# Two attention layers on one core: layer normalisation's last step and the first layer's low activation part moved from VectorE to GpSimd

## What is computed

```
def _layernorm(x, axis=-1, eps=1e-05):
    m = jnp.mean(x, axis=axis, keepdims=True)
    v = jnp.var(x, axis=axis, keepdims=True)
    return (x - m) / jnp.sqrt(v + eps)
...
    x = _layernorm(x + _L0_gnn_ref(x, adj, L0_gnn_Wq, L0_gnn_bq, L0_gnn_Wk, L0_gnn_bk, L0_gnn_Wv, L0_gnn_bv, L0_gnn_beta), axis=-1)
    x = _layernorm(x + _L1_gnn_ref(x, adj, L1_gnn_Wq, L1_gnn_Wk, L1_gnn_Wv, L1_gnn_bv, L1_gnn_Wo, L1_gnn_bo), axis=-1)
    return x
```

## Time and profile before

| | |
|---|---|
| median of 3 runs | 1102.79 us (1102.42 to 1103.21) |
| the profiled execution | 1102.04 us |
| its span on the core | 1100.2 us |
| busy: PE, DVE, POOL, ACT | 96%, 85%, 48%, 40% of the span |
| granted TensorE clock, mean | 0.992 of full speed |

### The profile page before, as it was taken

The page is one execution under the profiler, slowest core; times in us unless marked ns, Lnnn a source line. Parts: engine busy times, 40 slices in busy tenths (PEclk is TensorE's granted clock), DMA queues, the critical chain, the costliest instruction groups (busy, mean ns, idle before and its releaser), DMA issues.

```text
span 1100.2 us, 38267 instructions
## 1 busy us (share of the span) xinstructions
PE 1061.6 (96%) x16896; PEld 916.5 (83%) x16896; DVE 936.5 (85%) x1642; ACT 445.3 (40%) x713; POOL 529.2 (48%) x454
## 2 busy tenths in 40 slices
PE   6789999999999999999999999999999999999975
PEld 5678888888888888888888888888888888888864
DVE  4468998989989898898989989898998989878786
ACT  4334434433444344444434344343343434444321
POOL 0235554554545445364554645455364544655443
PEclk9899999999999999999999999999999999999998
DMA  8211211202111111211201111111211210010101
GB/s 271 64 40 36 74 31 49 60 20 61 38 43 59 43 38 46 65 38 43 59 30 51 46 40 56 42 42 42 65 38 43 59 41 11 17 36 2 36 29 37
DMA packets 61749, 53.32 MB, mean 48 GB/s; under 512 B 35984, under 2 KB 55440, under 8 KB 61584
## 3 DMA queue, kind: packets, MB, share of 16 engines
q1 hardware_dynamic: 60752, 49.69, 15.3%
q10 hardware_dynamic: 832, 1.18, 0.3%
HBM read 38.28 MB, written 12.58 MB: 46 GB/s over the span
## 4 chain that ended last, share of the span: by engine, by line
PE 90%; DVE 4%; issue 2%; ACT 1%; DMA 1%; POOL 1%; ACTq 0%; POOLq 0%; DVEq 0%
PE ps_u L346 53%; PE ps_s L363 9%; PE ps_o L346 8%; PE ps_p L431 7%; PE ps_p L446 7%; PE ps_x L376 3%; PE ps_o L460 2%; DVE probs L628 1%; POOL probs L766 1%; DMA k_sb<-in_wk 1%; DVE row_sum L678 1%; DVE xt_lo L656 1%; ACT probs L553 0%; DMA xt_in<-in_x_t 0%; DVE row_max L638 0%
## 5 line engine op out<-in xcount | busy, mean ns | idle before, releaser
L766 POOL TENSOR_TENSOR probs<-probs,row_max 128x768 f32<-128x768 f32 x128 | 209.8, 1639 | 314.9 <-DVE row_max L638 314.9
L772 POOL TENSOR_TENSOR probs<-probs,row_inv 128x768 f32<-128x768 f32 x128 | 188.9, 1475 | 127.1 <-DVE row_inv L686 69.2
L522 ACT COPY probs_t<-ps_p 128x768 f32<-128x768 f32 x128 | 102.7, 802 | 201.9 <-PE ps_p L431 201.8
L346 PE MATMUL ps_u<-w_hi_v,xt_lo 128*128 128x384 f32 x384 | 137.9, 359 | 5.0 <-DVE v_sb L671 5.0
L553 ACT ACTIVATE probs<-probs 128x768 f32<-128x768 f32 x128 | 108.3, 846 | 83.5 <-POOL probs L766 83.4
L678 DVE TENSOR_REDUCE row_sum<-probs 128x12 f32<-128x768 f32 x128 | 121.5, 949 | 23.9 <-ACT probs L553 23.1
L787 POOL TENSOR_TENSOR rstd<-var_eps,minus_half 128x1 f32<-128x1 f32 x128 | 70.3, 549 | 125.5 <-DVE var_eps L719 125.5
L346 PE MATMUL ps_u<-w_hi_v,xt_hi 128*128 128x384 f32 x384 | 129.7, 338 | 0.0
L346 PE MATMUL ps_u<-w_lo_v,xt_hi 128*128 128x384 f32 x384 | 129.3, 337 | 0.0
L346 PE MATMUL ps_u<-xt_hi,w_lo_k 128*128 128x512 f32 x288 | 119.1, 414 | 4.9 <-DVE v_sb L671 4.9
L346 PE MATMUL ps_u<-xt_hi,w_lo_q 128*128 128x512 f32 x285 | 121.7, 427 | 1.7 <-ACT q_sb L541 0.9
(11 more groups left out here) (78 smaller groups left out, 2031.3 us busy)
## 6 DMA issues: line engine op xcount, KB each, us to landing
x_in<-in_x SPq DMA_DIRECT2D x16, 768.0 KB, 4.6
out<-z SPq DMA_DIRECT2D x64, 192.0 KB, 1.9
xt_in<-in_x_t SPq DMA_DIRECT2D x15, 768.0 KB, 4.6
adj<-in_adj SPq DMA_DIRECT2D x64, 128.0 KB, 2.9
xt_in<-in_x_t SPq DMA_DIRECT2D x3, 256.0 KB, 4.7
q_sb<-in_wq ACTq DMA_DIRECT2D x3, 192.0 KB, 4.9
k_sb<-in_wk ACTq DMA_DIRECT2D x1, 576.0 KB, 7.9
v_sb<-in_wv SPq DMA_DIRECT2D x1, 576.0 KB, 7.7
```

Of the source, the lines that this page charges most:

```text
L346: last = nc.tensor.matmul(dst, a(g), b(g), start=(g == 0 and n == 0), stop=(g == KT - 1 and n == 2))
L522: nc.scalar.copy(probs_t[:].rearrange("p (a i) n -> p a (i n)", a=2), ps_p[:, :, 0:KT * P]).then_inc(probs_t_ready, 1)
L766: nc.gpsimd.tensor_tensor(s, s, over_keys(row_max[p]), ALU.subtract).then_inc(shifted, 1)
L772: nc.gpsimd.tensor_tensor(s, s, over_keys(row_inv[p]), ALU.mult).then_inc(probs_ready, 1)
```

## The change

`normalise` moves to POOL, directly behind the power of the same tile, so it comes one step earlier and POOL has it for both layers. `activations_lo` is divided: for the first layer POOL makes it, after the shift of the step, for the second layer DVE keeps it. The semaphore `xt_lo_ready` is split in two, one for each layer, with a count of its own (`low_no`). DVE gets a new wait: before it overwrites `z`, the normalisation of the first-layer tile that used the buffer two tiles earlier must be over.

```diff
-        xt_lo_ready = sem("xt_lo_ready")
+        xt_lo_ready = [sem(f"xt_lo_ready{l}") for l in range(2)]
...
-                    sp.wait_ge(xt_lo_ready, TURN_NO[0, c - 1, TILES - 1])
+                    sp.wait_ge(xt_lo_ready[0], low_no((0, c - 1, TILES - 1)))
...
-                    pe.wait_ge(xt_lo_ready, TURN_NO[layer, c, TILES - 1])
+                    pe.wait_ge(xt_lo_ready[layer], low_no((layer, c, TILES - 1)))
...
+                if earlier and earlier[0] == 0:
+                    dve.wait_ge(normed, at(earlier) + 1)
...
                 if s.cur:
                     bias_and_max(s.cur)
-                if s.done:
-                    normalise(s.done)
                 if s.turned:
                     activations_lo(s.turned)
...
+            def activations_lo(tile):
+                layer, c, t = tile
+                if layer == 1:
+                    return
+                p = home((layer, c))
+                pool.wait_ge(xt_hi_ready, TURN_NO[tile])
+                pool.wait_ge(xt_loaded, 16 * c)
+                cols = slice(t * P, (t + 1) * P)
+                nc.gpsimd.tensor_tensor(xt_lo[p][:, :, cols], xt_in[:, :, cols], xt_hi[p][:, :, cols].bitcast(F32),
+                                        ALU.subtract).then_inc(xt_lo_ready[0], 1)
...
+            def normalise(tile):
+                layer, c, t = tile
+                pool.wait_ge(rstd_ready, at(tile) + 1)
+                dst = x1[c % 3][:, t, :] if layer == 0 else z[t % 2][:]
+                nc.gpsimd.tensor_scalar(dst, z[t % 2][:], mean_var[t % 2][:, 0:1], rstd[t % 2][:],
+                                        ALU.subtract, ALU.mult).then_inc(normed, 1)
...
                 if s.turned:
                     add_bo(s.turned)
+                    activations_lo(s.turned)
                 if s.last:
                     inverse_deviation(s.last)
+                    normalise(s.last)
                 if s.cur:
                     scale(s.cur)
```

More of the change, by code:

```diff
@@ L89, in second_no, with low_no @@
     return TILES * tile[1] + tile[2] + 1
+def low_no(tile):
+    return TILES * (tile[1] - (tile[0] == 0)) + tile[2] + 1
 def tile_before(tile, n):
@@ L373, in turn_activations @@
                 pe.wait_ge(normed, at((0, c, t)) + 1)
-                pe.wait_ge(xt_lo_ready, TURN_NO[tile] - 1)
+                if low_no(tile) > 1:
+                    pe.wait_ge(xt_lo_ready[1], low_no(tile) - 1)
                 for g in range(KT):
@@ L638, in bias_and_max @@
                 nc.vector.tensor_reduce(row_max[t % 2][:], rows, AX_X, ALU.max).then_inc(max_ready, 1)
[L640 to L645, removed]
             def activations_lo(tile):
                 layer, c, t = tile
+                if layer == 0:
+                    return
                 p = home((layer, c))
                 dve.wait_ge(xt_hi_ready, TURN_NO[tile])
[L651 to L658, removed]
+                cols = slice(t * P, (t + 1) * P)
+                nc.vector.tensor_tensor(xt_lo[p][:, :, cols], ps_x[:, 0:D].rearrange("p (g n) -> p g n", g=KT),
+                                        xt_hi[p][:, :, cols].bitcast(F32), ALU.subtract).then_inc(xt_lo_ready[1], 1)
             def unit_out(unit):
```

## The result

The changed kernel takes 1088.39 us (median of 4 runs, 1087.25 to 1089.26), the kernel before, run beside it on the same chip, 1103.0 us (1102.42 to 1103.3): a ratio of 0.9875, 95% interval 0.9863 to 0.9887, so faster by 1.25%. The prediction said 1088. The profiled execution took 1088.4 us with a span of 1086.5, which is 13.7 us less than the span of before.

What follows compares the result with a forecast made beforehand. It took PE as the bound (busy 96%), with gains only where PE waits: start 10.6, middle 3.2, end 0.9 less 0.2, together 14.5 us. From 1102.04 that gave 1087.5, predicted as 1088 us, range 1083 to 1098.

Steps and rivals of the forecast that it cites:

- The sum of 14.5 us: Whole kernel: gains of 10.6 at the start, 3.2 in the middle, 0.9 at the end, less 0.2 lost there.
- First gap: PE's wait at 32.20 us: `v_sb` comes earlier, a key unit runs inside the gap, 2.2 us stay; gain 4.6 us.
- the rival of half clock: Start: PE still falls to half clock in the first step and after the fourth gap; about 1092 us, chance 0.16.
- The choice of the full level: First step: PE's unit behind the remaining 2.2 us gap runs at full clock, gaining 4.6 us; at half clock 2.5.
- Second and third gap: PE's waits at 45.07 and 54.96 us: low parts in front of `v_sb` leave DVE; gains 0.5 and 1.2 us.
- Fourth gap: PE's wait at 68.03 us falls from 3.83 to 1.6, and the lowered clock behind it need not follow; gain 3.9 us.
- Fifth gap: PE's wait at 104.13 us: the low part is second-layer, so only `normalise` leaves DVE; gain 0.4 us.
- The start: Before 110 us: PE's five waits for DVE's copy of a value unit shrink, together 10.6 us.
- The middle: PE's loads wait 15 times for POOL's scaling; scaling 0.6 us earlier removes 15 x 0.21 = 3.2 us.
- The estimate of normalise on POOL: `normalise` on POOL takes 0.7 us, scaled from a select; between 0.3 and 1.0 it moves only the last 0.3.
- The end: From 1051.63 us: five shifts each 0.17 us shorter gain 0.9; POOL's slower `normalise` behind the last power loses 0.2.
- POOL blocks DVE in return: Rival: POOL's `normalise` holds up DVE's small product, so second-layer scaling is late, 13 x 0.4 = 5.2 us; 1093 us, chance 0.10.

Runs made afterwards that it cites:

- hi_late: The whole change, with ACT's rounded copy of tile (0, 2, 0) put behind the q and k copies in the first step; 1086.15 us, ratio 0.9855.
- scale_first: The whole change, but POOL scales before it normalises; 1085.78 us, ratio 0.985 to the kernel before.
- low_only: Against the whole change, `normalise` is back on VectorE, so only the first layer's low part is on GpSimd; 1085.57 us, ratio 0.9852.
- dose_half: The whole change, with a second GpSimd instruction of normalise's form on 192 columns ahead of each `normalise`; 1105.24 us, ratio 1.0027.
- norm_only: Against the whole change, the low part is back on VectorE, so only `normalise` is on GpSimd; 1092.25 us, ratio 0.9913.
- low_hi_late: low_only, with ACT's rounded copy of tile (0, 2, 0) put behind the q and k copies in the first step; 1083.04 us, ratio 0.9828.

## Why the prediction was right, point by point

The direction and the cause hold: on VectorE a block ended, and the start and the middle became shorter by it. The sum of 14.5 us came out as 13.7, or 13.0 without the shift of the first scores, but its terms didn't come out alike: the start was taken 3.4 us too high, the middle 3.5 too low, the end had the wrong sign. That 1088 us met the measured time to 0.4 us is therefore luck.

- **First gap, 4.6 us; measured 2.6.** `v_sb` did come earlier and the first key unit ran inside the old gap, and the gap left, 2.75 us, is near the 2.2 that I gave. But the clock fell behind it (0.91 from 25 to 45 us), so in this step the rival of half clock happened, for which the working gave 2.5. hi_late, where the gap is gone, has granted clock 1.00 there and the second tile 4.6 us earlier. The choice of the full level was the step that failed here.
- **Second and third gap, 0.5 and 1.2; measured 0.5 and 1.5.** Right, to 0.3 us.
- **Fourth gap, 3.9; measured 3.5.** The gap is 1.70 us (1.6 predicted), and the clock stayed at 1.00.
- **Fifth gap, 0.4; measured 0.4.** It fell from 0.73 to 0.35 us. But two new waits for scaling, 0.23 us before it and 1.40 behind it, took 1.8 us away (0.4 and 1.4). These are the price of POOL's dear `normalise`; scale_first has only 0.10 us of them. At tile 10 another 0.56 us came in, where PE waited for scaling before (0.37 us at 116.26). The start: 7.2 instead of 10.6 us.
- **The middle, 3.2; measured 6.7.** The lead rises at two places in each chunk, by 0.28 and 0.25 us. The first is the wait for scaling that I priced (13 times 0.28 is 3.6). The second I overlooked: in the trace of before PE's loads also wait 13 times for ACT's `k_sb`, which stands behind an exponential that the late shift of a chunk's first second-layer tile holds up (the row below). The shift is late since the bias ahead of it is: behind the blocked low part, then for 1.50 us beside POOL's scaling, where it now takes 0.41. The second part alone doesn't make the wait: in low_only the bias step still takes 1.51 us at the median, and the wait for `k_sb` is gone. The one cause, DVE's delay, was in my working; I followed it to scaling only. The waits of the kernel before have the row, total us, times, longest; those of after have none for `k_sb` in the middle:

```profile
PEld ps_u L346 <- ACT k_sb L543: 2.9, 13, 0.2
```

- **The estimate of normalise on POOL, 0.7 us, bounds 0.3 to 1.0; measured 1.65.** This step failed. I scaled it from a select and bounded it by a two-input add, and took for granted that one tensor operand cannot cost more than two. That "0.7 fits" in POOL's idle time was thus wrong, and scaling does begin behind `normalise`. The prediction held that unknown costs move the sum by little; this one took 1.8 us at the start, about 1 in the middle (0.08 us per chunk, by scale_first) and 1.2 at the end. The change still gains because DVE's share comes earlier by more than that. By dose_half another 1.0 us is more than is left.
- **The end, +0.9 and -0.2; measured +0.1 and -1.0.** The shift fell to 1.47 us and the steps from 1051.50 to 1065.62 are 7.06 us apart instead of 7.23, but the loop's entry lost the gain again: the lead falls by 0.2 us at tile 125, and it is 13.89 at tile 122 and 14.00 at the last. Which instruction lost it no run shows. The last term is mis-sized by the same 1.65 us.
- **POOL blocks DVE in return.** Not seen: the small product (L682) takes 171 ns at the median and 174 at most.
- **What the two parts share.** My working gave the low part's 1.83 us to the shift beside it, which is right, and the 0.47 of `normalise` only its own length. norm_only shows that `normalise` was what made the low part late for the ports; so the two gains overlap, and low_only is faster than the whole change, by 2.5 us by the ratios, whose intervals just touch.

## What to carry to other kernels

Where two engines lock each other out, look at which one starts first, by tenths of a microsecond: a short instruction in front of a block can cost the whole block, and taking away either it or the blocked one clears it, so price them together and not as a sum. Price an operation on an engine where it has no row by a probe or by wide bounds, since a form with fewer operands isn't bound by one with more, and find the point from which it decides. And follow a delay to every engine that waits behind it: half of the middle's gain here was in a wait that I had not followed.

## What was not expected of the hardware

- GpSimd's operation with two scalars for 128x384 took 1.65 us, with one 1.17 to 1.24, but a tensor operation with the column spread over the row 0.83 us. The cost didn't halve with the columns: 1.00 us for 192.
- A gap of about 2 us was followed by half clock in one kernel and not in another. Granted clock over 45 to 70 us in low_only, behind a gap of 2.09 us at 60.75, and in low_hi_late, behind one of 2.04 at 58.86:

```profile
45.00:70.00 25.00, 22.91 (x299) 20.53 (x299) 18.68 (x34) 9.08 (x14) 11.79 (x11) 0.93 0.17 45
```

```profile
45.00:70.00 25.00, 22.96 (x328) 19.97 (x332) 18.62 (x34) 10.46 (x16) 13.30 (x12) 1.00 0.16 45
```

  In low_only the gap at 32 us had already been followed by half clock; in low_hi_late the granted clock was 1.00 from 25 us on. What decides stays open.
- The landing of the one DMA on which the first gap hangs differs between executions: where ACT's copy behind it kept its place, it starts between 29.96 us (whole change) and 31.91 (norm_only), and the first gap varies with it: 2.75 us in the whole change, 4.28 in dose_half, which does the same work up to there. A term of the start read from one execution is uncertain by as much.
